# A graph network's first pass over the edges: a batch's sums are added in four quarters between VectorE's compares

## The chip, the cores and the metric

The kernel runs on one core of one Trainium2 chip. The metric is the device time of one execution in microseconds, the median of several runs. The core has TensorE (PE, with weight loads shown apart as PEld), VectorE (DVE), ScalarE (ACT), GpSimd (POOL) and SyncE (SP), which mostly issues DMAs.

## What is computed

Four layers of a graph network run one after the other over 6250 nodes with 64 features and 200000 edges, sorted by target node. The first one is the one that matters here:

```python
h = jnp.maximum(_layernorm(x, axis=-1), 0.0)
msg = jnp.concatenate([h[src], edge_features], axis=1)      # 200000 x 96
agg = jax.ops.segment_sum(msg, dst, num_segments=6250)
x = x + relu(jnp.concatenate([h, agg], axis=1) @ W.T + b)
```

The second and the fourth layer are attention layers over the same edges, the third one a weighted sum. The first layer's pass over the edges also builds two tables of one-hots (of a source node's low and high part) that the third layer reads later.

## The kernel before

The edges are cut into 392 batches of 512 (four tiles of 128). `sum_sweep` is the first layer's pass. Each engine runs its own list of stages through `pipeline(eng, stages, unroll)`: at step t it does, in the order of the list, each stage (lag, stage) for batch t - lag. Two times 16 steps are written out, the rest is a loop of 16 steps a turn, and the last steps are written out again. So the order of the list is the order of the engine's instructions, and a wait in a stage holds all that stands behind it.

In a step the engines do this:

- POOL (`gather_stage`, L780): four indirect DMAs fetch the rows of a batch's 512 source nodes into one of 8 buffers, once PE has summed the batch that used the buffer before. One batch in eight (`looked_up`, slot 3) needs none, since its rows come from the look-up below.
- ScalarE: `join` (L1055) puts the edge features beside the rows; `hots` (L1072, L1076) makes the node one-hots of 17 tiles of nodes.
- PE: `sums` (L1092) adds up the batch with four f32 matmuls, in one of four PSUM banks, then `lookups` (L1100): for every eighth batch the rows are found by one-hot matmuls instead of a gather, spread over eight batches. A batch has four look-ups with one-hots of VectorE and two of ScalarE (three in one slot), in this order: two of VectorE, one of ScalarE, two of VectorE, one of ScalarE. Each look-up is four matmuls.
- VectorE: `build` (L1131) compares the target nodes of batch t; `low` (L1152) and `high` (L1161) make batch t - 2's part of the tables for later; `add` (L1141) takes batch t - 6's sums from PSUM and adds them to 128 columns of `accT` in SBUF, at a window whose start is in a register; `hots` (L1176) makes four node one-hots for batch t - 6's look-ups; `fill` (L1190) reduces the two banks of a finished look-up, in one step of eight.
- SP: loads of edge features (L1005), of the source lines that `low` reads (L1014), of the indices (L791), of the look-up line (L1040), and the store of the tables (L1024). `line` and `keep` wait for `low` and `high`.

`add` and the four `hots` are of the same batch: PE's look-ups of batch b need hots(b), these stand behind add(b), and add(b) waits for PE's sums(b). The four hots have four buffers, and each waits until PE has used the one before it in its buffer.

VectorE's list before is

```python
pipeline(dve, [(0, build), (2, low), (2, high), (6, add), (6, hots), (7, fill)], unroll=GATHER_UNROLL)
```

Of the kernel before, what the change touches and what calls it, by code (L numbers as in the profile page):

```python
# [19 lines left out]


# [1 line left out]

# [1 line left out]

# [7 lines left out]
ALU = mybir.AluOpType  # L33
# [24 lines left out]
WINDOW, WINDOW_STEP = 128, 64  # L58
# [9 lines left out]
LOOK_EVERY, LOOK_AT = 8, 3  # L68
# [4 lines left out]
GATHER_UNROLL = 2 * IDX_GROUP  # L73
# [48 lines left out]
def done(eng, sem, b):  # L122

    eng.wait_ge(sem, b.v + 1)


def free(eng, sem, b, ring):

    if not b.early(ring):
        eng.wait_ge(sem, b.v + (1 - ring))  # L130
# [28 lines left out]
def pipeline(eng, stages, unroll=UNROLL):  # L159

    def step(i, t):
        for lag, stage in stages:
            b = t - lag
            if i is not None or 0 <= b < N_BATCHES:
                stage(Batch(i, b, unroll))
    last = (N_BATCHES - 1) // unroll
    for t in range(2 * unroll):
        step(None, t)
    with eng.bass.Fori(2, last, engines=(eng.engine,), head_slot={eng.engine: 0}) as i:
        for u in range(unroll):  # L170
            step(i, u)
    for t in range(last * unroll, N_BATCHES + max(lag for lag, _ in stages)):
        step(None, t)
# [63 lines left out]
def graph_layers(nc, a, out):  # L237
    ctx = contextlib.ExitStack()
    with ctx:
        def sb(name, shape, dt=F32):  # L240
# [44 lines left out]
        accT = wide_room[:, 0:N_PAD]  # L285
# [105 lines left out]
        dve_bases, dve_late_bases, pe_bases = (  # L391
            Bases(eng, name, base) for eng, name in ((nc.vector, "now"), (nc.vector, "late"),
                                                     (nc.tensor, "pe")))
# [521 lines left out]
        def sum_sweep(name):  # L915


            width = sum_width

            def sweep():  # L920
                with Phase(nc, name) as ph:
                    s_onehot, s_joined, s_sum, s_added, s_low, s_high = (
                        ph.sem(n) for n in ("onehot", "joined", "summed", "added", "low", "high"))
# [37 lines left out]
                    def onehots_of(b):  # L961
                        slot = b.slot(SUM_RING)
                        t = onehot if slot < RING else onehot_wide
                        return t[:, slot % RING, :, :]

                    def sum_bank(b):
                        return banks[b.slot(RING)][0:width, 0:P]
# [10 lines left out]
                    def hots_dve(b):  # L978
                        n = HOTS_DVE // LOOK_EVERY
                        return range(n * b.slot(LOOK_EVERY), n * (b.slot(LOOK_EVERY) + 1))  # L980
# [9 lines left out]
                    @block.gpsimd  # L990
                    def _(pool):
                        pipeline(pool, [(0, gather_stage(pool, node_rows, sum_rows[:, :, :, 0:D], s_rows, s_idx,
                                                         [s_sum], some_looked_up=True))],
                                 unroll=GATHER_UNROLL)
                        end_gathers(pool, some_looked_up=True)
# [130 lines left out]
                    @block.vector  # L1126
                    def _(dve):
                        def build(b):
                            free(dve, s_sum, b, SUM_RING)
                            wide = [P, TILES_PER_BATCH, P]  # L1130
                            dve.tensor_tensor(  # L1131
                                onehots_of(b), iota[:, :].unsqueeze(1).to_broadcast(wide),
                                tiles_of(dst_rel, b).unsqueeze(2).to_broadcast(wide),
                                ALU.is_equal).then_inc(s_onehot, 1)

                        def add(b):
                            at = accT[0:width, bass.ds(dve_bases.of(b), WINDOW)]
                            done(dve, s_sum, b)
                            if not b.early(1):
                                dve.wait_ge(s_added, b.v)  # L1140
                            dve.tensor_tensor(at, sum_bank(b), at, ALU.add).then_inc(s_added, 1)  # L1141

                        def hot_of(b):
                            return hot_out[:, b.of_group(EDGE_GROUP).slot(2), b.slot(EDGE_GROUP), :]

                        def low(b):
                            slot = b.of_group(EDGE_GROUP).slot(2)
                            landed(dve, s_line, b.of_group(EDGE_GROUP), 16)
                            if not b.early(2 * EDGE_GROUP):
                                dve.wait_ge(s_kept[slot], b.of_group(EDGE_GROUP).uses(2) * 16)  # L1150
                            wide = [P, BATCH // 2, 2]
                            dve.tensor_tensor(  # L1152
                                hot_of(b)[:, 0:BATCH].rearrange("p (e t) -> p e t", t=2),
                                low_line[:, slot, b.slot(EDGE_GROUP), :].rearrange(
                                    "p (e t) -> p e t", t=2),
                                lane_pair[:, :, :].to_broadcast(wide),
                                ALU.is_equal).then_inc(s_low, 1)

                        def high(b):
                            wide = [P, TILES_PER_BATCH, NODE_TILES]  # L1160
                            dve.tensor_tensor(  # L1161
                                hot_of(b)[:, BATCH:HOT].rearrange("p (g j) -> p g j", j=NODE_TILES),
                                iota_b[:, 0:NODE_TILES].unsqueeze(1).to_broadcast(wide),
                                tiles_of(src_high, b).unsqueeze(2).to_broadcast(wide),
                                ALU.is_equal).then_inc(s_high, 1)
                        def hots(b):
                            if not has_lookup(b):
                                return
                            if b.slot(LOOK_EVERY) == 0:
                                landed(dve, s_look, b.of_group(LOOK_EVERY), 16)  # L1170
                            before = block_of(b) * HOTS_DVE
                            for n in hots_dve(b):
                                if n >= 4 or not b.early(LOOK_EVERY):
                                    dve.wait_ge(s_used_dve, before + n - 3)
                                wide = [P, BATCH // 2, 2]
                                dve.tensor_tensor(  # L1176
                                    dve_hots[:, n % 4, :].rearrange("p (e t) -> p e t", t=2),
                                    look_in(b).rearrange("p (e t) -> p e t", t=2),
                                    node_pairs[:, n:n + 1, :].to_broadcast(wide),
                                    ALU.is_equal).then_inc(s_hot_dve, 1)  # L1180

                        def fill(b):
                            if b.slot(LOOK_EVERY) != LOOK_EVERY - 1 or not has_lookup(b):
                                return
                            to = b.later(LOOK_AT + 1)
                            dve.wait_ge(s_used_dve, (block_of(b) + 1) * HOTS_DVE)
                            dve.wait_ge(s_used_act, (block_of(b) + 1) * HOTS_ACT)
                            dve.wait_ge(s_sum, to.v + (1 - ROW_RING))
                            for h, bank in enumerate(look_banks(b)):
                                last = dve.reduce_sum(  # L1190
                                    sum_rows[:, LOOK_AT, 2 * h:2 * h + 2, 0:D],
                                    bank[:, 0:2 * PARTS * D].rearrange(
                                        "p (g n d) -> p g d n", n=PARTS, d=D), AX)
                            last.then_inc(s_filled, 1)
                        c = Chain(dve, s_parts)
                        for tiles in src_groups:
                            value = of_tiles(normed, tiles)
                            left = parts_left.rearrange("p (j d) -> p j d", d=D)[:, 0:len(tiles), :]
                            parts = [parts_of(tiles)[:, :, n, :] for n in range(PARTS)]
                            c.do(split(dve, c, value, left, parts))  # L1200
                        pipeline(dve, [(0, build), (2, low), (2, high), (6, add), (6, hots), (7, fill)],
                                 unroll=GATHER_UNROLL)
            windows_loop(name, sweep, [next_places])

        def kept_sum_sweep(name):
# [946 lines left out]
        low, high = slice(0, WINDOW_STEP), slice(WINDOW_STEP, P)  # L2152
# [172 lines left out]
```

## Time and profile before

| what | value |
|---|---|
| time, median of 3 runs | 7310.23 us (7301.25 to 7313.19) |
| span of the profiled execution | 8677.5 us |
| PE busy in the span | 4986.1 us, 57% |
| DVE busy | 4776.9 us, 55% |
| ACT busy | 4214.7 us, 49% |
| POOL busy | 5500.0 us, 63% |
| mean granted TensorE clock | 0.733 |

The profile is of one execution, whose span is 1367 us longer than the median of the timed runs. Busy time leaves out register, branch, semaphore and DMA-issuing instructions of all engines but POOL's indirect DMAs. In a timeline a row merges like instructions that follow one another; the bracket behind it is the engine's idle time before it and what ended it. "issue" is time in which the engine waited for nothing that the profile shows, "remote" a wait whose releaser it does not find.

### The profile page before, as it was taken

To read this page: it belongs to the slowest core of one execution; us is meant where nothing else is said; L and a number is where in the kernel's file an instruction comes from. 1 tells how busy PE (TensorE), PEld (TensorE's weight loads), DVE (VectorE), ACT (ScalarE), POOL (GpSimd) and SP (SyncE) were. 2 spreads that over 40 slices of the span, in tenths; PEclk is the share of its full clock that TensorE was granted. 3 is DMA by queue.
4 is the path that set the end of the run, shared out by engine and by line. 5 is a ranking of instruction groups with operands and counts; after the bars stand their busy time and mean duration, and the time that the engine had idled before them with its cause. 6 is when DMAs were issued, how large, how long until landed. Compare 5 with 4: busy or idle time off the path is not lost. (4 is left out here: it accounts for less than half of the span.)

```text
span 8677.5 us, 161248 instructions
## 1 busy us (share of the span) xinstructions
PE 4986.1 (57%) x37998; PEld 3663.8 (42%) x38194; DVE 4776.9 (55%) x21264; ACT 4214.7 (49%) x11640; POOL 5500.0 (63%) x5713
## 2 busy tenths in 40 slices
PE   4555555555564444444444447997566666666664
PEld 3455444554452222222222226885444444444443
DVE  5455444554444555555455558996555555555556
ACT  3455444554423433333333348994455554544544
POOL 6777777777745555555555556994555555555553
PEclk8788888888776666666666668998666666666666
DMA  3232322333224444444444446885222222222221
GB/s 113 79 85 84 85 78 84 85 84 85 78 77 128 128 127 125 126 124 128 124 125 128 126 130 195 268 268 211 57 60 62 62 62 61 60 61 61 62 61 43
DMA packets 672779, 908.53 MB, mean 105 GB/s; under 512 B 141174, under 2 KB 429928, under 8 KB 672441
## 3 DMA queue, kind: packets, MB, share of 16 engines
q1 hardware_dynamic: 502366, 605.50, 22.6%
q0 software_dynamic: 168944, 301.30, 14.2%
q8 instruction: 42, 0.69, 0.0%
q10 hardware_dynamic: 1357, 0.47, 0.0%
q14 instruction: 70, 0.57, 0.0%
HBM read 696.57 MB, written 210.28 MB: 105 GB/s over the span
## 5 line engine op out<-in xcount | busy, mean ns | idle before, releaser
L780 POOL DMA_INDIRECT rows<-src_rows,idx_slots x1563 | 1489.5, 953 | 1214.6 <-DVE pre L1487 667.1
L780 POOL DMA_INDIRECT rows<-node_rows,idx_slots x1371 | 1867.1, 1362 | 569.0 <-issue 363.9
L780 POOL DMA_INDIRECT rows<-rel_rows,idx_slots x1563 | 1482.7, 949 | 1093.8 <-remote 457.3
L1375 ACT ACTIVATE onehot<-ident,fresh_slots 128x128 f32<-128x128 f32 x3136 | 992.6, 387 | 969.1 <-remote 651.8
L1366 PE MATMUL bank<-onehot,ones 128*128 128x512 f32 x1568 | 1296.2, 922 | 114.5 <-ACT onehot L1375 52.6
L1100 PE MATMUL bank<-by_chunk,dst_pairs 128*128 128x192 bf16 x6144 | 714.8, 265 | 973.9 <-DVE dst_pairs L1176 716.1
L1463 PE MATMUL bank<-w_e,edge_in 128*128 128x256 f32 x784 | 442.0, 665 | 1403.0 <-DVE onehots L860 1070.7
L1072 ACT ACTIVATE dst_pairs<-pre,minus_node 128x512 bf16<-128x512 int16 x816 | 580.8, 720 | 1220.5 <-remote 660.3
L1100 PEld LDWEIGHTS bank<-by_chunk,dst_pairs 128*128 128x128 bf16 x6144 | 534.8, 105 | 1084.0 <-DVE dst_pairs L1176 783.6
L1463 PEld LDWEIGHTS bank<-w_e,edge_in 128*128 128x128 f32 x784 | 192.3, 299 | 1853.9 <-DVE onehots L860 887.1
L1141 DVE TENSOR_TENSOR wide_room<-bank,wide_room 96x128 f32 x392 | 112.6, 287 | 1258.5 <-remote 719.0
L1512 DVE TENSOR_TENSOR onehots<-bank,onehots 128x512 f32<-128x512 f32 x392 | 269.7, 688 | 936.6 <-remote 669.3
L1669 PE MATMUL bank<-rows,onehot 128*128 128x65 f32 x3136 | 599.2, 352 | 243.2 <-DVE wide_room L1762 205.6
L1609 ACT ACTIVATE shrink<-grown 128x1 f32<-128x1 f32 x392 | 79.5, 203 | 1215.0 <-DVE grown L1713 974.8
L1669 PEld LDWEIGHTS bank<-rows,onehot 128*128 128x128 f32 x3136 | 553.1, 265 | 259.9 <-issue 240.7
L1446 ACT ACTIVATE onehot<-onehots,exp_bias 128x512 bf16<-128x512 f32 x392 | 282.9, 722 | 677.7 <-DVE max_by_chunk L1544 286.4
L1176 DVE TENSOR_TENSOR dst_pairs<-pre,node_pairs 128x512 bf16<-128x512 int16 x1536 | 544.6, 414 | 0.0
L1076 ACT ACTIVATE dst_pairs<-dst_pairs,ones 128x512 bf16<-128x512 bf16 x816 | 540.7, 707 | 1.6
L1624 ACT ACTIVATE onehot<-onehots,edge_in 128x128 f32<-128x128 bf16 x1568 | 500.6, 389 | 20.0
L1294 ACT ACTIVATE onehot<-onehots,edge_scale 128x128 f32<-128x128 bf16 x1568 | 500.7, 390 | 12.6 <-DVE onehots L1349 12.5
L1100 PE MATMUL bank<-wide_room,dst_pairs 128*128 128x192 bf16 x3264 | 439.4, 261 | 35.0 <-ACT dst_pairs L1076 30.3
L1643 PEld LDWEIGHTS bank<-by_chunk,onehots 128*128 128x128 bf16 x3136 | 269.2, 125 | 417.4 <-issue 416.8
(304 smaller groups left out, 11860.9 us busy)
## 6 DMA issues: line engine op xcount, KB each, us to landing
edge_in<-dst_line SPq DMA_DIRECT2D x392, 256.0 KB
spill<-rows SPq DMA_DIRECT2D x392, 256.0 KB
rows<-spill SPq DMA_DIRECT2D x392, 256.0 KB, 3.2
hot_rows<-rows SPq DMA_DIRECT2D x98, 712.0 KB
onehots<-hot_rows SPq DMA_DIRECT2D x196, 356.0 KB, 3.5
onehots<-src_low SPq DMA_DIRECT2D x98, 512.0 KB
edge_in<-in_ea_l SPq DMA_DIRECT2D x98, 256.0 KB
edge_in<-in_eaT_l SPq DMA_DIRECT2D x392, 64.0 KB
```

The source lines that it names most:

```text
L780: pool.indirect_dma_start(out=to[:, b.slot(ROW_RING), g, :], out_offset=None, in_=table, in_offset=bass.IndirectOffsetOnAxis(ap=idx_slots[ ...
L1072: act.activation(act_hots[:, n % 2, :], look_in(b), ACT.Square, bias=minus_node[:, n:n + 1]).then_inc(s_square, 1)
L1076: act.activation(act_hots[:, n % 2, :], act_hots[:, n % 2, :], ACT.Relu, scale=-1.0, bias=ones[:, 0:1])\
L1100: last = pe.matmul(look_banks(b)[g // 2][:, at:at + PARTS * D], hot[:, g * P:(g + 1) * P], node_parts(j), start=(j == 0 and g % 2 == 0), s ...
L1176: dve.tensor_tensor(dve_hots[:, n % 4, :].rearrange("p (e t) -> p e t", t=2), look_in(b).rearrange("p (e t) -> p e t", t=2), node_pairs[:, ...
L1294: last = act.activation(onehot[:, b.slot(RING), g, :], plain_of(b)[:, g, :], ACT.Copy, scale=edge_scale[:, b.slot(RING), g:g + 1])
L1366: return pe.matmul(bank, ones[:, :], diag[:, b.slot(2), :, :].rearrange("p g e -> p (g e)"), start=start, stop=True)
L1375: last = act.activation(diag[:, b.slot(2), g, :], ident[:, :], ACT.Copy, scale=fresh_slots[:, b.slot(2 * RING), g:g + 1])
L1446: act.activation(exp_out, masked1[:, b.slot(2), :], ACT.Exp, bias=exp_bias[:, slot, :], accum_out=exp_sum[:, slot, :])
L1463: pe.matmul(to, edge_blocks[:, b.slot(RING), :], w1_e[:, :, :].rearrange("p g f -> p (g f)"), start=True, stop=False)
L1624: last = act.activation(weighted[:, b.slot(2), g, :], onehot_b[:, b.slot(ONEHOT_RING), g, :], ACT.Copy, scale=share[:, b.slot(RING), g:g + 1])
L1669: last = pe.matmul(summed, weighted[:, b.slot(2), g, :], rows[:, b.slot(ROW_RING), g, D:2 * D + 1], start=(g == 0), stop=(g == TILES_PER_B ...
```

## The change

`add` is cut into four instructions of 32 columns each, and `hots` into four stages of one compare each. The list of VectorE becomes: build(t), add0, hot0, add1, hot1 (all of t - 6), low(t - 2), add2, hot2, high(t - 2), add3, hot3, fill(t - 7). The wait for PE's sums stands at the first quarter, the semaphore `s_added` is raised by the last one. Nothing else is changed.

```diff
+                        added_at = [0]
+
+                        def add(b, quarter):
+                            n = WINDOW // 4
+                            if quarter == 0:
+                                added_at[0] = dve_bases.of(b)
+                                done(dve, s_sum, b)
+                                if not b.early(1):
+                                    dve.wait_ge(s_added, b.v)
+                            at = accT[0:width, bass.ds(added_at[0] + quarter * n, n)]
+                            last = dve.tensor_tensor(
+                                at, sum_bank(b)[:, quarter * n:(quarter + 1) * n], at, ALU.add)
+                            if quarter == 3:
+                                last.then_inc(s_added, 1)
...
-                            for n in hots_dve(b):
+                            for n in hots_dve(b)[which:which + 1]:
...
-                        pipeline(dve, [(0, build), (2, low), (2, high), (6, add), (6, hots), (7, fill)],
-                                 unroll=GATHER_UNROLL)
+                        pipeline(dve, [(0, build), (6, add0), (6, hot0), (6, add1), (6, hot1), (2, low),
+                                       (6, add2), (6, hot2), (2, high), (6, add3), (6, hot3),
+                                       (7, fill)], unroll=GATHER_UNROLL)
```

## Rows read from the trace of the kernel before

**Rows 1.** Windows: stretch, its length, each engine's busy time, PEclk, DMA share, GB/s

```profile
82.00:2481.00 2399.00, 1340.62 (x12536) 1205.50 (x12536) 1140.52 (x3184) 1158.03 (x2012) 1850.88 (x1354) 0.82 0.30 83
...
2626.00:5231.00 2605.00, 1222.29 (x6191) 640.30 (x6187) 1344.01 (x7394) 1034.75 (x3119) 1447.79 (x1519) 0.64 0.46 126
...
6101.00:8607.00 2506.00, 1558.34 (x10335) 1097.96 (x10529) 1359.83 (x8592) 1274.31 (x4300) 1452.46 (x1531) 0.68 0.23 61
```

**Rows 2.** The page's groups: busy, mean ns of one, idle before and releaser

```profile
L780 POOL DMA_INDIRECT rows<-src_rows,idx_slots x1563 | 1489.5, 953 | 1214.6 <-DVE pre L1487 667.1
```

**Rows 3.** Groups of instructions in 300 to 2300 us, inside the first layer's pass

```profile
L780 POOL DMA_INDIRECT rows<-node_rows,idx_slots x1144 | 1536.4, 1343 | 463.4 <-issue 300.2 <-PE bank L1092 83.1 <-remote 80.2
...
L1141 DVE TENSOR_TENSOR wide_room<-bank,wide_room 96x128 f32 x323 | 92.8, 287 | 1053.3 <-remote 655.4 <-PE bank L1092 329.3 <-issue 68.5
```

**Rows 4.** Timelines of DVE, PE and POOL, one quick turn: start, us, instruction, [idle before]

```profile
1223.70 0.29 DVE L1141 TENSOR_TENSOR wide_room<-bank,wide_room 96x128 f32 x1 [1.01 <-PE bank L1092]
1223.91 1.42 DVE L1176 TENSOR_TENSOR dst_pairs<-pre,node_pairs 128x512 bf16<-128x512 int16 x4
1225.25 0.68 DVE L1131 TENSOR_TENSOR onehots<-iota,dst_rel 128x512 f32<-128x512 f32 x1
1225.85 0.41 DVE L1152 TENSOR_TENSOR rows<-onehots,lane_pair 128x512 bf16<-128x512 bf16 x1
1226.19 0.36 DVE L1161 TENSOR_TENSOR rows<-iota_b,src_high 128x200 bf16<-128x200 bf16 x1
1227.55 0.29 DVE L1141 TENSOR_TENSOR wide_room<-bank,wide_room 96x128 f32 x1 [1.00 <-PE bank L1092]
...
1224.38 0.84 PE L1100 MATMUL bank<-by_chunk,dst_pairs 128*128 128x192 bf16 x8 [0.81 <-DVE dst_pairs L1176]
...
1226.38 1.04 PE L1092 MATMUL bank<-onehots,rows 128*96 128x128 f32 x8
...
1223.82 0.94 POOL L780 DMA_INDIRECT rows<-node_rows,idx_slots  x1 [0.30 <-PE bank L1092]
1225.07 2.29 POOL L780 DMA_INDIRECT rows<-node_rows,idx_slots  x1 [0.31 <-issue]
```

**Rows 5.** Timeline ahead of the loop, when PE waits for rows

```profile
163.69 0.29 DVE L1141 TENSOR_TENSOR wide_room<-bank,wide_room 96x128 f32 x1 [3.59 <-issue]
...
164.96 2.39 POOL L780 DMA_INDIRECT rows<-node_rows,idx_slots  x1 [0.30 <-issue]
...
166.18 0.36 DVE L1161 TENSOR_TENSOR rows<-iota_b,src_high 128x200 bf16<-128x200 bf16 x1
...
170.19 0.29 DVE L1141 TENSOR_TENSOR wide_room<-bank,wide_room 96x128 f32 x1 [3.65 <-issue]
```

**Rows 6.** Timeline at a standstill of the loop

```profile
1269.34 0.29 DVE L1141 TENSOR_TENSOR wide_room<-bank,wide_room 96x128 f32 x1 [2.60 <-PE bank L1092]
...
1272.03 1.04 PE L1092 MATMUL bank<-onehot,rows 128*96 128x128 f32 x8
...
1285.85 0.29 DVE L1141 TENSOR_TENSOR wide_room<-bank,wide_room 96x128 f32 x1 [12.72 <-remote]
```

**Rows 7.** Timeline of a step with reductions behind the hots, 16 batches earlier

```profile
1170.98 0.29 DVE L1141 TENSOR_TENSOR wide_room<-bank,wide_room 96x128 f32 x1 [2.61 <-PE bank L1092]
1171.19 1.43 DVE L1176 TENSOR_TENSOR dst_pairs<-pre,node_pairs 128x512 bf16<-128x512 int16 x4
...
1172.00 1.11 POOL L780 DMA_INDIRECT rows<-node_rows,idx_slots  x1 [0.30 <-issue]
```

**Rows 8.** VectorE's timeline in an attention pass: short additions

```profile
3805.05 0.15 DVE L1535 TENSOR_TENSOR grown<-max_by_chunk,run_max 128x1 f32<-128x1 f32 x1
3805.11 0.15 DVE L1537 TENSOR_TENSOR top<-run_max,a_b 128x1 f32<-128x1 f32 x1
3805.18 0.35 DVE L860 TENSOR_SCALAR onehots<-edge_in,window_lane 128x512 bf16<-128x512 int16 x1
```

**Rows 9.** Window of the stretch in which PE waits for rows

```profile
157.00:177.00 20.00, 11.47 (x98) 9.81 (x96) 8.83 (x26) 9.83 (x18) 16.34 (x13) 0.91 0.16 44
```

More of the change, by code:

```diff
@@ L22 @@
 import contextlib
+import functools
 import numpy as np
@@ L1134, in build @@
                                 ALU.is_equal).then_inc(s_onehot, 1)
[L1136 to L1141, printed above, removed]
+                        added_at = [0]
[11 more added lines that the diff above has]
+                                last.then_inc(s_added, 1)
                         def hot_of(b):
@@ L1165, in high, with hots @@
                                 ALU.is_equal).then_inc(s_high, 1)
-                        def hots(b):
+                        def hots(b, which):
                             if not has_lookup(b):
                                 return
-                            if b.slot(LOOK_EVERY) == 0:
+                            if b.slot(LOOK_EVERY) == 0 and which == 0:
                                 landed(dve, s_look, b.of_group(LOOK_EVERY), 16)
                             before = block_of(b) * HOTS_DVE
-                            for n in hots_dve(b):
+                            for n in hots_dve(b)[which:which + 1]:
                                 if n >= 4 or not b.early(LOOK_EVERY):
@@ L1200, in _ @@
                             c.do(split(dve, c, value, left, parts))
-                        pipeline(dve, [(0, build), (2, low), (2, high), (6, add), (6, hots), (7, fill)],
-                                 unroll=GATHER_UNROLL)
+                        add0, add1, add2, add3 = (functools.partial(add, quarter=n)
+                                                  for n in range(4))
+                        hot0, hot1, hot2, hot3 = (functools.partial(hots, which=n)
+                                                  for n in range(4))
+                        pipeline(dve, [(0, build), (6, add0), (6, hot0), (6, add1), (6, hot1), (2, low),
+                                       (6, add2), (6, hot2), (2, high), (6, add3), (6, hot3),
+                                       (7, fill)], unroll=GATHER_UNROLL)
             windows_loop(name, sweep, [next_places])
```

## The prediction, made before the result was known

> **What bounds the kernel now.** I read the windows by stage first [rows 1]. The first layer's pass is the stretch 82 to 2481 us: 2399 us for 392 batches, 6.12 us a batch, and no engine is full in it (POOL 77% busy, PE 56%, DVE 48%). The two attention passes follow and nothing of them is touched. Two limits lie in this pass, and a third thing that is neither: standstills.
>
> The first limit is a ring between TensorE and VectorE. In the timeline of an undisturbed batch [rows 4] the reader is to follow one turn: the add at 1223.70 waits for PE's sums; the four node compares (hots) start 0.21 later; PE's look-ups start at 1224.38, when the first compare is there; they and the next sums keep PE busy until 1226.38 + 1.04 = 1227.42; the next add starts at 1227.55. A turn is 3.85 us. VectorE idles 1.00 of it, PE 0.81.
>
> The second limit is POOL, which issues a batch's row gathers: four a batch, none for every eighth batch, so 56 for 16 batches. One that nothing holds takes 0.94 and 0.30 pass before the next: 1.25 us, or 3.5 x 1.25 = 4.38 us a batch. Yet of the gathers in [rows 4] one takes 0.94 and the next 2.29. The second starts at 1225.07 in the last hot and ends at 1227.36, which is 0.81 after the end of the compare "high" (1226.19 + 0.36 = 1226.55); the 2.39 one in [rows 5] ends at 167.35, again 0.81 after high's end (166.54). So a gather whose start meets VectorE's unbroken run of hots, build, low and high (2.64 us, 1223.91 to 1226.55) is held until that run is over. The mean gather of this pass is 1343 ns, not 944 [rows 3]. In the ordinary turn POOL gets two gathers through in 3.85 us, while 3.5 a turn are wanted: the eight buffers of rows run empty. Once they are empty the batch looks as in [rows 5]: add to add 6.50 us (163.69, 170.19), PE waiting for rows, three gathers at 1.25 and one at 2.69 (2.39 + 0.30), together 6.44. That is this pass when POOL bounds it: 14 batches of 16 have gathers, 14 x 6.50 / 16 = 5.69 us a batch.
>
> The third thing is a standstill. In [rows 6] PE's sums start at 1272.03 and the profile has them take 1.04, but the add that waits for them starts at 1285.85, with 12.72 of idle put down to "remote". Of 1053 us that VectorE idles ahead of the add in 2000 us, 655 are put down to "remote" [rows 3], in most turns of the loop two waits in each 16 batches, at the same place. Sixteen batches take 1269.34 - 1170.98 = 98.4 us (6.15 each): some fourteen quick turns and two of 16 to 22 us. In these POOL catches up, so in the profile it is not the bound that it would be without them.
>
> **Are the standstills in the timed runs?** The timed median is 7310, the profiled span 8677.5, 1367 longer; something of the profile is not in the runs. Take the attention passes at POOL's own pace, 392 x 4 gathers x 1.25 (mean 0.95 [rows 2] and 0.30 between [rows 4]) = 1960 us each instead of 2605 and 2506. The rest of the span outside the three passes is 8677 - 2399 - 2605 - 2506 = 1167. There is left for the first pass 7310 - 1167 - 3920 = 2223 us, 5.67 a batch. That is what [rows 5] gave for a pass bound by POOL with no standstill (5.69). It is one fit and no proof, but I take it: in the timed runs POOL bounds the first pass.
>
> **The change, part by part.** *The add in quarters.* One add of 128 columns takes 0.29 and lets the next instruction start after 0.21 [rows 4]. The nearest rows below are additions of one column, 0.15 long with the next starting 0.06 to 0.07 later [rows 8]. Between them a quarter of 32 columns occupies 0.07 + (32/128) x 0.14 = about 0.10; bounds 0.07 and 0.21. Four are 0.42 instead of 0.21 (0.28 to 0.84), while VectorE has 1.00 idle in the quick turn and more in the slow one: the extra 0.2 costs nothing by itself. The base of the window is read once a batch as before, and the semaphore is raised by the last quarter.
>
> *The order.* Before: add, four hots, build, low, high. After: add0, hot, add1, hot, low, add2, hot, high, add3, hot, then build. This is in PE's ring, since PE wants the hots one after the other. From the add's start as zero, with steps of 0.335 (hot, low), 0.29 (high), 0.10 (quarter), 0.41 for a hot's length and 0.06 until PE has it [rows 4]: hots reach PE at 0.57, 1.01, 1.78 and 2.50. A look-up lasts 0.33 (six of them lie between 1224.38 and the sums at 1226.38). PE does hot 1 until 0.90, waits 0.11, does hot 2 and ScalarE's first until 1.67, waits 0.11, does hot 3 until 2.11, waits 0.39, does hot 4 and ScalarE's second until 3.16, then the sums until 4.20, and 0.13 to the next add: 4.33 us instead of 3.85. So the ring itself gets 0.48 longer. With quarters at 0.07 it is 4.2, at 0.21 4.8.
>
> *What lies behind the moved wait.* add0 waits for PE and now has low and high queued behind it, which went ahead of it before. SP's loads and stores (L1005, L1014, L1024, L791) wait for them, so they go out up to 3 us later. The lines that low reads are fetched four batches ahead and the indices too, some 17 us: covered, and if not, POOL would wait for indices. build keeps its place at the head of a step, six batches before its reader.
>
> *POOL's holds.* The one run of 2.64 us falls into four: hot (0.34), hot and low (0.67), hot and high (0.62), hot and build (0.94). Whether a held gather gets in at such a break is seen in [rows 7], the batch in which two reductions of a PSUM bank follow the hots: the gather of 1172.00 takes 1.11 and ends at 1173.11; 0.81 back is 1172.30, the end of the third hot and before the fourth is over (1172.62). With an instruction in the queue that reads only one tensor of SBUF, POOL gets in soon. The add is of that kind: gathers that start beside it take 0.94 (1223.82 in [rows 4]). A gather that starts at a random point of a turn of about 4.9 waits on average (0.34² + 0.67² + 0.62² + 0.94²) / (2 x 4.9) = 0.18 us; 3.5 of them 0.63. POOL then needs 4.38 + 0.63 = 5.0 us a batch; bounds 4.4 (no wait) and 5.69 (as before).
>
> **Sum.** POOL 5.0 against the ring's 4.33: POOL still bounds, 5.69 - 5.0 = 0.69 us a batch saved, 392 x 0.69 = 270 us: 7310 - 270 = 7040. If POOL needed no wait the ring (4.33) and POOL (4.4) would give 1.3 x 392 = 510, so 6800; PE's clock speaks against that end. In [rows 9] PE is busy 11.47 of 20 us and the granted clock is 0.91 of the higher level (2.4 GHz), so with pauses it already drops at times to 1.2 GHz; after the change PE is busy 3.03 of 5.0, 61%, and some batches will still run at the lower level, where PE's 3.03 become about 6.
>
> **Rules of the Trainium skill.** The rows show holds over a whole run of instructions. "SBUF — State Buffer", who interferes with whom, says that a VectorE instruction with two SBUF inputs contends with a GpSimd instruction that reads SBUF, and one with a single SBUF input does not; it also says the loser blocks until the instruction ends. By the first the trace agrees, and the change helps. By the second, taken alone, a gather would get in after each compare already; [rows 4] differ from that (held over four instructions). The page adds that tensor_tensor was not seen to stall DMA issue; the 2.29 us gather here says otherwise.
>
> **Rivals.** *B, the standstills are in the timed runs.* For it: they sit at the same place in every turn of the loop, which looks like the program and not like the recording. Then they are POOL's time to catch up, POOL is not the bound, and the ring's 0.48 is lost in each batch: 392 x 0.48 = +188, 7310 + 188 = 7500; somewhat less, 7460, where a longer turn shortens them. It decides once the two standstills are longer than about 22 us together in 16 batches: (16 x 4.33 + 22) / 16 = 5.7, the batch of before. Against it: the fit above. The Trainium skill's page "Runtime: NRT & Kernel Launch", instruction fetch mechanics, says a taken branch to code outside the fetched window stalls the engine; by that rule they would be real. *C, POOL is not let in.* The breaks are only about 0.1 long, a compare is queued behind each, and the gather waits for the end of build. Then the blocked run grows from 2.64 to 0.32 + 0.335 x 5 + 0.29 + 0.60 = 2.9 and the held batch from 6.50 to 6.75: 0.25 x 14/16 x 392 = +85, 7395. Against it: [rows 7]. *D, standstills of middle length (12 to 22 us in 16 batches).* Gain and loss cancel: -100 to +40.
>
> **Chances.** Forecast (A) 0.55; B 0.25; C 0.10; D 0.10. Range: A reaches from 6900 (4.65 a batch) to 7170, B to 7480: 6900 to 7480. A alone: 6900 to 7170. A measurement of this kernel tells about 0.2% (15 us) from no change. Faster by more: 0.55 of A and half of D, 0.60. Within: 0.05. Slower: B, C and a part of D, 0.35.
>
> **What would show it.** In the profile after: gathers of L780 near 1.0 to 1.1 us in the mean instead of 1343 ns (step POOL; still 1.3 or more means C). Quick turns of 4.33 in place of 3.85, with PE idle put down to L1176 in three places (step order). L780 with short waits for PE's sums, because its eight buffers are full earlier. If the standstills are still in the profile and only there, its span gets longer (16 x 0.48 = 7.7 us in 98.4) though the timed runs get shorter; if both get longer, it is B. A quarter over 0.2 us apart or a clock that stays at the lower level would put the time above the forecast.

## The result, and the profile after

Before takes 7308.89 us (median of 20 runs, 7290.22 to 7330.5), the changed kernel 7321.65 us (20 runs, 7308.02 to 7328.81). The ratio is 1.0018, 95% interval [1.0011, 1.0025]: slower by 13 us, 0.18%. The forecast was 7040. The time lies outside the range of the forecast's own case (A, 6900 to 7170), and inside the whole range (6900 to 7480) only because that was stretched for rival B, which is not what happened.

First the windows of the profile after, the three passes (columns as in [rows 1]):

```profile
82.00:2397.00 2315.00, 1610.28 (x12495) 1301.65 (x12496) 1225.03 (x4332) 1161.99 (x2012) 1904.95 (x1346) 0.84 0.31 86
2535.00:4655.00 2120.00, 1360.56 (x7838) 718.57 (x7839) 1472.21 (x7707) 1152.46 (x3520) 1588.91 (x1780) 0.70 0.64 173
5340.00:7250.00 1910.00, 1390.05 (x10174) 982.59 (x10365) 1302.48 (x8443) 1253.61 (x4228) 1434.18 (x1517) 0.78 0.30 79
```

The span is 7322.3 us, 1355 less than that of before's first profile, and all three passes are shorter than in [rows 1]. (The second and third stretch do not fit the attention passes closely: these last from 2513 to 4464 and from 5305 to 7243 us.) That is no work of the change. A new profile of the kernel before (the first experiment) has a span of 7317.3 us. The standstills of [rows 6] were in that one execution and not in the timed runs beside it, and the two new profiles are what may be compared. Their groups in 300 to 2300 us (columns as in [rows 3]), first before, then after:

```profile
L780 POOL DMA_INDIRECT rows<-node_rows,idx_slots x1177 | 1643.9, 1397 | 358.8 <-issue 353.0 <-PE bank L1092 5.8
...
L1100 PE MATMUL bank<-by_chunk,dst_pairs 128*128 128x192 bf16 x5369 | 686.7, 282 | 274.7 <-DVE dst_pairs L1176 274.7
...
L1141 DVE TENSOR_TENSOR wide_room<-bank,wide_room 96x128 f32 x336 | 96.6, 287 | 1006.5 <-PE bank L1092 1006.5
```

```profile
L781 POOL DMA_INDIRECT rows<-node_rows,idx_slots x1165 | 1646.6, 1413 | 355.0 <-issue 352.3 <-PE bank L1093 2.7
L1101 PE MATMUL bank<-by_chunk,dst_pairs 128*128 128x192 bf16 x5308 | 740.0, 282 | 318.6 <-DVE dst_pairs L1185 317.3
...
L1147 DVE TENSOR_TENSOR wide_room<-bank,wide_room 96x32 f32 x1328 | 241.0, 181 | 895.5 <-PE bank L1093 894.1
```

In both POOL is never without work: its gathers are 0.30 us apart, and only 3 to 6 of 2000 us are waits for PE. It sets the pace with 3.5 x (1.40 + 0.30) = 5.95 us a batch before and 3.5 x (1.41 + 0.30) = 6.0 after. From build to build a batch takes 5.96 us before and 6.01 after (mean of batches 60 to 370). The change did not shorten the gathers. Its other half is there: PE waits 318.6 instead of 274.7 us for the hots.

### The profile page after: what moved, and what is told of

It is laid out like the page before. It is cut to its first block and busy times, and to the rows that moved or that the text cites. A ratio compares the mean times of both kernels' runs of the same rounds, so it can differ in the third digit from the quotient of the medians.

```text
span 7322.3 us, 163600 instructions
## 1 busy us (share of the span) xinstructions
PE 5119.7 (70%) x37998; PEld 3629.9 (50%) x38194; DVE 4811.0 (66%) x22440; ACT 4195.7 (57%) x11640; POOL 5568.7 (76%) x5713
## 5 line engine op out<-in xcount | busy, mean ns | idle before, releaser
L781 POOL DMA_INDIRECT rows<-node_rows,idx_slots x1371 | 1929.4, 1407 | 439.5 <-issue 413.5
L1380 PE MATMUL bank<-onehot,ones 128*128 128x512 f32 x1568 | 1251.2, 893 | 132.2 <-ACT onehot L1389 123.9
L1101 PE MATMUL bank<-by_chunk,dst_pairs 128*128 128x192 bf16 x6144 | 857.4, 282 | 369.9 <-DVE dst_pairs L1185 368.5
L1147 DVE TENSOR_TENSOR wide_room<-bank,wide_room 96x32 f32 x1568 | 283.7, 182 | 1052.9 <-PE bank L1093 1051.2
L1185 DVE TENSOR_TENSOR dst_pairs<-pre,node_pairs 128x512 bf16<-128x512 int16 x1536 | 636.5, 414 | 7.0 <-issue 6.3
L1683 PE MATMUL bank<-rows,onehot 128*128 128x65 f32 x3136 | 538.6, 327 | 48.5 <-DVE wide_room L1776 46.3
L1501 DVE TENSOR_TENSOR pre<-bank,rows 128x256 f32<-128x256 f32 x392 | 165.9, 423 | 573.1 <-DMA rows<-src_rows,idx_slots 569.6
L1683 PEld LDWEIGHTS bank<-rows,onehot 128*128 128x128 f32 x3136 | 495.2, 240 | 64.4 <-issue 54.3
L1101 PE MATMUL bank<-wide_room,dst_pairs 128*128 128x192 bf16 x3264 | 476.4, 279 | 1.8 <-ACT dst_pairs L1077 0.6
L1699 DVE CUSTOM_DVE_ANT_0 pre<-bank,rows 128x64 f32<-128x64 f32 x1568 | 259.9, 221 | 318.0 <-DMA rows<-rel_rows,idx_slots 313.4
```

What stands on the lines that cost most here:

```text
L781: pool.indirect_dma_start(out=to[:, b.slot(ROW_RING), g, :], out_offset=None, in_=table, in_offset=bass.IndirectOffsetOnAxis(ap=idx_slots[ ...
L1101: last = pe.matmul(look_banks(b)[g // 2][:, at:at + PARTS * D], hot[:, g * P:(g + 1) * P], node_parts(j), start=(j == 0 and g % 2 == 0), s ...
L1147: last = dve.tensor_tensor(at, sum_bank(b)[:, quarter * n:(quarter + 1) * n], at, ALU.add)
L1185: dve.tensor_tensor(dve_hots[:, n % 4, :].rearrange("p (e t) -> p e t", t=2), look_in(b).rearrange("p (e t) -> p e t", t=2), node_pairs[:, ...
L1380: return pe.matmul(bank, ones[:, :], diag[:, b.slot(2), :, :].rearrange("p g e -> p (g e)"), start=start, stop=True)
L1683: last = pe.matmul(summed, weighted[:, b.slot(2), g, :], rows[:, b.slot(ROW_RING), g, D:2 * D + 1], start=(g == 0), stop=(g == TILES_PER_B ...
```

## Where a gather gets in

DVE's and POOL's timelines of a quick turn in the profile after, to be held against [rows 4]:

```profile
1204.21 0.19 DVE L1147 TENSOR_TENSOR wide_room<-bank,wide_room 96x32 f32 x1 [1.30 <-PE bank L1093]
1204.32 0.42 DVE L1185 TENSOR_TENSOR dst_pairs<-pre,node_pairs 128x512 bf16<-128x512 int16 x1
1204.66 0.18 DVE L1147 TENSOR_TENSOR wide_room<-bank,wide_room 96x32 f32 x1
1204.77 0.41 DVE L1185 TENSOR_TENSOR dst_pairs<-pre,node_pairs 128x512 bf16<-128x512 int16 x1
1205.10 0.41 DVE L1161 TENSOR_TENSOR rows<-onehots,lane_pair 128x512 bf16<-128x512 bf16 x1
...
1206.58 0.68 DVE L1132 TENSOR_TENSOR onehot<-iota,dst_rel 128x512 f32<-128x512 f32 x1
1208.56 0.19 DVE L1147 TENSOR_TENSOR wide_room<-bank,wide_room 96x32 f32 x1 [1.31 <-PE bank L1093]
...
1205.28 2.79 POOL L781 DMA_INDIRECT rows<-node_rows,idx_slots  x1 [0.30 <-issue]
1208.38 0.94 POOL L781 DMA_INDIRECT rows<-node_rows,idx_slots  x1 [0.30 <-issue]
```

The turn is 4.35 us (1204.21 to 1208.56), predicted 4.33; a quarter and the compare behind it are 0.11 apart, predicted 0.10. But the gather of 1205.28 ends at 1208.07, and 0.81 back is 1207.26 = 1206.58 + 0.68, the end of build. It waited through the rest of low, two hots, high, two quarters and build. The reader can see why the quarter is no break: the first hot ends at 1204.32 + 0.42 = 1204.74, the quarter started at 1204.66, before that end, and the next hot starts at 1204.77. Between the two compares lie 0.03 us (0.02 in most places; without a quarter the next compare starts 0.08 before the end of the one ahead, [rows 4]). In 300 to 2300 us, 324 of before's 1176 gathers take 1.5 us or more (mean 2.56), and 318 of the 1165 after (mean 2.59). Between 1.0 and 1.5 us there are 31 before and 118 after: mostly gathers that started in the first hot and got in at its end, or in build, behind which VectorE is idle.

For the question at which boundary between two compares a waiting gather gets in, I took every gather of 1.03 us or more that starts in 300 to 1800 us and counted the ends of compares that it waited through and the one at which it got in (its own end less 0.81). Ends within 0.10 us of a gather's start are left out, and so is the end of a run, behind which VectorE is idle. Of the changed kernel and the four kernels made from it the table has only the boundaries with something between the compares; where two compares still overlap in them, 2 gathers got in and 434 ends were waited through (changed) and 15 and 675 (quarters alone). By the gap, from the end of one compare to the start of the next:

| kernel | gap and what is in it | got in | waited on |
|---|---|---|---|
| before, again | -0.08, nothing | 15 | 907 |
| changed | 0.02 to 0.03, a quarter | 36 | 376 |
| quarters alone | 0.02 to 0.03, a quarter | 84 | 152 |
| before, waits behind 6 compares | 0.03, VectorE waits | 146 | 0 |
| the same | 0.12 to 0.22, VectorE waits | 213 | 0 |
| before, waits behind the hots | 0.03 to 0.27, VectorE waits | 364 | 0 |
| the same | -0.08, nothing | 53 | 0 |
| before, waits behind build and low (a run with standstills, below) | 0.03 to 0.04, VectorE waits | 191 | 0 |
| the same | -0.08, nothing | 16 | 697 |
| changed, copy 96x32 | 0.12, quarter and copy | 257 | 2 |
| changed, copy 96x128 | 0.22, quarter and copy | 260 | 0 |
| changed, second add | 0.22, quarter and second add | 255 | 0 |

## Experiments

Where nothing else is said the result is unchanged by the edit. The mean gather and the us a batch (build to build, batches 60 to 370) are from each profile, gathers in 500 to 1500 us.

| kernel | us, before beside it | ratio, 95% interval | mean gather, ns | us a batch |
|---|---|---|---|---|
| before, again | 7319.13, 7301.57 | one run | 1394 | 5.96 |
| changed | 7321.65, 7308.89 | 1.0018 [1.0011, 1.0025] | 1413 | 6.01 |
| quarters alone | 7261.12, 7301.57 | 0.994 [0.9927, 0.9952] | 1389 | 5.91 |
| order alone | 7318.25, 7301.57 | 1.0021 [1.0012, 1.003] | 1419 | 6.03 |
| before, waits behind 6 compares | 6784.98, 7301.57 | 0.9288 [0.9274, 0.9301] | 1020 | 4.64 |
| before, waits behind the hots | 6783.37, 7315.99 | 0.9271 [0.9256, 0.9287] | 1006 | 4.60 |
| changed, copy 96x32 in 3 breaks | 7002.56, 7311.59 | 0.9574 [0.9558, 0.959] | 1179 | 5.17 |
| changed, copy 96x128 in 3 breaks | 7108.05, 7315.99 | 0.9715 [0.9698, 0.9731] | 1266 | 5.51 |
| changed, second add in 3 breaks | 7101.31, 7311.59 | 0.9712 [0.9696, 0.9728] | 1261 | 5.49 |
| changed, waits behind hots, low, high | 7170.59, 7311.59 | 0.9809 [0.9792, 0.9825] | 988 | 5.68 |

**The kernel before, once more**, to see whether the standstills belong to it.

> The kernel before once more, unchanged, for a profile. If the standstills of the first profile belonged to that execution alone, the span is about 7310 us, the first pass lasts about 2220 us, gathers of the pass take about 1.4 us in the mean and the steady batch is 6.5 us from add to add. If they belong to the program, two of 16 to 22 us stand in each 16 batches again.

Span 7317.3 us, no idle time put down to "remote" ahead of the add (the row above; it was 655.4 in [rows 3]), 5.96 us a batch. POOL bounds the first pass, as the forecast's fit had said; rival B, which needed the standstills in the timed runs, falls for these runs.

**The change's two parts, one at a time.** Quarters alone: the list is build, low, high, add0, hot0, add1, hot1, add2, hot2, add3, hot3. Order alone: add stays whole.

```diff
-  pipeline(dve, [(0, build), (2, low), (2, high), (6, add), (6, hots), (7, fill)],
+  pipeline(dve, [(0, build), (6, add), (6, hot0), (6, hot1), (2, low),
+                 (6, hot2), (2, high), (6, hot3), (7, fill)],
```

> Quarters alone: build, low and high keep their old place ahead of the add; the four quarters alternate with the four hots. Theory Q (a held gather waits for every compare that VectorE's queue already holds, and a quarter between them does not let it in): the run that holds a gather grows by three quarters of 0.10, the time stays or rises by up to 0.3 x 14/16 x 392 = 100 us. Theory G (the quarters let gathers in, the new order ate the gain): faster by 100 us or more, mean gather below 1.2 us.

> Order alone: the add stays whole, low and high go between the hots. Theory Q: the run that holds a gather keeps its 2.64 us, POOL still bounds, within 20 us of before. Theory G (order costs PE's ring 0.4 us a batch): slower by more than 60 us.

Quarters alone are 40 us faster, which neither of its theories had; order alone is 17 slower, as theory Q said; the sum would be -23 and both together are +13, so they are not additive. Neither moves the mean gather by more than 25 ns. With the quarters alone, 49 gathers of 500 to 1500 us, which started in the first hot, end 0.81 behind its end (mean 1.05 us), but of the 159 that started in a later hot 132 are held to the end of high (2.1 to 3.2 us) and 26 to the end of the last hot.

**VectorE waits for its own compare**, in the order of before, behind hots, build and low, then behind the hots only. The edit puts a real gap between two compares:

```diff
                                     ALU.is_equal).then_inc(s_hot_dve, 1)
+                                dve.wait_ge(s_hot_dve, before + n + 1)
...
                                 ALU.is_equal).then_inc(s_onehot, 1)
+                            done(dve, s_onehot, b)
...
+                            done(dve, s_low, b)
```

> The kernel before with a wait of VectorE for its own last compare behind every hot, build and low, so that the next compare is not in its queue while one runs. Theory Q: a gather gets in after one compare at most, mean gather about 1.1 us, the pass needs about 5.0 us a batch instead of 5.7, some 200 us faster, if VectorE's waits (some 0.1 each, 0.7 a batch) do not bound. Theory L (the port is held from the first to the last compare whatever is queued, or the gather waits for VectorE's idleness for another reason): gathers as before, time as before or up to 100 us slower.

> The kernel before with the waits behind the four hots only; build, low and high still follow one another unbroken (1.3 us). Theory Q: a gather that comes in the hots is let in after one, one that comes in the last compares waits for the end of high, up to 1.3: mean gather 1.1 to 1.2, time between drained (6785) and before (7302), near 6900.

Minus 7.1 and minus 7.3%, more than either expectation had. The shorter gathers account for it: 3.5 x (1.394 - 1.020) = 1.31 us a batch with six waits, against 5.96 - 4.64 = 1.32, so nothing is left for the clock to explain. Groups of the kernel with six waits, 500 to 1500 us, and its timeline:

```profile
L780 POOL DMA_INDIRECT rows<-node_rows,idx_slots x756 | 770.8, 1020 | 230.4 <-issue 226.7 <-PE bank L1092 3.7
...
L1142 DVE TENSOR_TENSOR wide_room<-bank,wide_room 96x128 f32 x216 | 61.9, 287 | 101.4 <-PE bank L1092 101.2
```

```profile
843.70 1.79 DVE L1178 TENSOR_TENSOR dst_pairs<-pre,node_pairs 128x512 bf16<-128x512 int16 x4
845.63 0.69 DVE L1131 TENSOR_TENSOR onehots<-iota,dst_rel 128x512 f32<-128x512 f32 x1
...
843.93 0.99 POOL L780 DMA_INDIRECT rows<-node_rows,idx_slots  x1 [0.30 <-issue]
845.23 1.07 POOL L780 DMA_INDIRECT rows<-node_rows,idx_slots  x1 [0.30 <-issue]
```

The hots end at 845.49 and build starts at 845.63, 0.14 later; between two hots the gap is 0.03, and four of them take 1.79 instead of the 1.42 of [rows 4], 0.12 more for each wait between them. No gather of the pass takes 1.5 us any more: the longest wait is for the end of the compare in progress. So the holds were what the forecast took them for, and worth more than it thought (517 and 533 us). What the change lacked was a gap that lets them in.

With the waits behind the hots only, build, low and high still overlap, and the expectation had gathers held there to the end of high. Yet of the gathers that started in build 53 got in at an overlapped end. So a gap behind the compare is not always needed.

Which gathers get in at a gap of 0.02 to 0.03 with a quarter in it can be told more closely. A gather that started in the first hot behind VectorE's idle time got in at its end each time (25 of 25 in the changed kernel, 79 of 79 with quarters alone). All others got in at such a gap 16 times and waited through it 528 times. In the kernel before, where the second hot overlaps the first, the gathers that started in the first compare behind idle time got in at its end in 4 of 50 cases. That is a pattern of these traces, not a cause shown.

**The ring by itself.** Before and the changed kernel, both with one gather a batch in the first pass instead of four; PE's sums then take the rows of the first tile for all four, so the first layer's sums are others.

```diff
-        return TILES_PER_BATCH
+        return GATHERED[0]     # 1 in sum_sweep("sum0")
...
-                                last = pe.matmul(sum_bank(b), sum_rows[:, b.slot(ROW_RING), g, :],
+                                last = pe.matmul(sum_bank(b), sum_rows[:, b.slot(ROW_RING), 0, :],
```

> The kernel before with one gather a batch in the first pass instead of four (all four sum matmuls read the first tile's rows, so the first layer's sums are of other rows). POOL then needs 1.25 to 2.7 us a batch and cannot bound. Step 'order' of the prediction: turns of 3.85 us from add to add.

> The changed kernel with one gather a batch, likewise. Step 'order': turns of 4.33 us, 0.48 longer than those of ring_before, with PE waiting for the hots in three places; the pass 392 x 0.48 = 190 us longer than that of ring_before. If the ring were not touched by the order, both passes are alike.

6548.62 and 6755.61 us, one run each: 207 us or 0.53 a batch for the change (predicted 0.48 and 188). Batches take 4.03 and 4.57 us, ordinary turns 3.85 and 4.35. The second kernel's timeline of PE has the waits where the prediction put them. Each row joins the matmuls of one look-up or two, so the waits show in the starts: the first two look-ups take 0.93 instead of the 0.84 of [rows 4], and those of the third and the fourth hot start 0.43 and 0.71 after the row ahead where 0.33 would do. That is 0.09, 0.10 and 0.38, predicted 0.11, 0.11 and 0.39:

```profile
1226.01 0.93 PE L1104 MATMUL bank<-by_chunk,dst_pairs 128*128 128x192 bf16 x8 [0.73 <-DVE dst_pairs L1188]
1226.78 0.49 PE L1104 MATMUL bank<-wide_room,dst_pairs 128*128 128x192 bf16 x4
1227.21 0.51 PE L1104 MATMUL bank<-by_chunk,dst_pairs 128*128 128x192 bf16 x4
1227.92 0.50 PE L1104 MATMUL bank<-by_chunk,dst_pairs 128*128 128x192 bf16 x4 [0.21 <-DVE dst_pairs L1188]
```

**How long must a break be, and of what kind?** The changed kernel with one more instruction behind quarters 2, 3 and 4, into unused SBUF: a copy of 96x32 from PSUM, a copy of 96x128, or a maximum of 96x128 that reads PSUM and SBUF.

```diff
+                            if quarter:
+                                last = dve.tensor_copy(
+                                    parts_left[0:width, quarter * P:(quarter + 1) * P], sum_bank(b))
```

> The changed kernel with a copy of the whole bank (96 x 128, PSUM to SBUF) behind the second, third and fourth quarter: breaks of 0.10 us become about 0.31. Theory Q (the compares already queued count): gathers are still held to the end of build; the run is 0.6 longer, so time rises by 0.6 x 14/16 x 392 = 200 us or up to it. Theory W (the break was only too short): mean gather falls from 1.41 to 1.15 or less and the time does not rise.

> The changed kernel with the copy of 96x32 behind three quarters, once more. Its gathers were 1198 ns in the mean, 1266 with the copy of 96x128. Without standstills it should then be the faster of the two: 0.955 to 0.97 against 0.9715 (6980 to 7090). If the length is what helps, it is above 0.975. With standstills 0.98 to 0.99 again.

> The changed kernel with a second 96x128 addition-like instruction (a maximum, PSUM and SBUF in) behind three quarters, once more. Its gathers were 1260 ns, as with the copy of the same size (1266), so without standstills the same ratio as there, 0.97 to 0.98 (7080 to 7150). If what reads SBUF holds POOL longer, 0.99 to 1.00. With standstills 0.985 to 0.995 again.

DVE and POOL of the kernel with the short copy:

```profile
1206.19 0.41 DVE L1164 TENSOR_TENSOR rows<-onehots,lane_pair 128x512 bf16<-128x512 bf16 x1
1206.53 0.18 DVE L1147 TENSOR_TENSOR wide_room<-bank,wide_room 96x32 f32 x1
1206.63 0.18 DVE L1150 COPY rel_biases<-bank 96x32 f32<-96x32 f32 x1
1206.73 0.41 DVE L1188 TENSOR_TENSOR dst_pairs<-pre,node_pairs 128x512 bf16<-128x512 int16 x1
...
1206.34 1.26 POOL L781 DMA_INDIRECT rows<-node_rows,idx_slots  x1 [0.30 <-issue]
```

low ends at 1206.60, the next hot starts at 1206.73: a gap of 0.13, and the gather gets in at the end of the copy (0.81 back from its end at 1207.60 is 1206.79; with the long copy and the maximum it is the end of the quarter, 0.09 behind the compare's). The same quarters with 0.02 to 0.03 between the compares let in few. So three instructions of 0.10 a batch turn 1.0018 into 0.957, without any wait. The long copy and the maximum, with gaps of 0.22, give the same time as each other (0.9715, 0.9712; gathers 1266 and 1261 ns): whether the filler reads one tensor of SBUF or none makes no difference. Longer than needed is worse, by some 100 us. One reason is in sight, though not tested alone: the fillers stand in the ring, and the phase of the requests shifts so that with the long copy 133 gathers in 500 to 1500 us start in the last hot and are held to the end of build (1.76 us each), which is the one place left without a gap.

**Both: the changed kernel with waits** behind each hot, low and high.

> The changed kernel with the waits behind hots, low and high, once more, for a comparison in which before takes near 7300. If the ring of the change bounds once the holds are gone: 4.7 to 5.2 us a batch, 6830 to 7000, ratio 0.935 to 0.96, against the 0.929 of the kernel before with waits. If POOL bounds both: 0.927 to 0.930. With standstills (before over 8500) 1.013 to 1.016 again.

```profile
L781 POOL DMA_INDIRECT rows<-node_rows,idx_slots x616 | 608.7, 988 | 389.6 <-PE bank L1093 208.8 <-issue 180.8
...
L1101 PE MATMUL bank<-by_chunk,dst_pairs 128*128 128x192 bf16 x2828 | 366.6, 254 | 346.4 <-DVE dst_pairs L1187 345.8 <-issue 0.7
```

The gathers are nearly as short as unheld ones (988 ns), yet the kernel is 386 us slower than the kernel before with its waits (0.9809 against 0.9288 of before), and slower than expected. POOL now waits 208.8 us in 1000 for PE, and PE 345.8 for the hots: the ring bounds, with ordinary turns of 5.39 us. Its timeline shows a quarter and a hot every 0.67 us, which were 0.44 apart without the waits, because a quarter can no longer start ahead of the end of the compare before it. The change's longer ring is a second loss, which POOL's holds cover in the changed kernel. By itself it is the 207 us of the ring test; the rest of the 386 comes with the waits, which lengthen this ring more than that of before.

**Comparisons in which the standstills are there.** In two of the comparisons the kernel before itself took 8558.82 us (14 runs, 8526.14 to 8586.11) and 8655.81 us (7 runs, 8642.54 to 8670.59), near the span of the first profile. It is not a matter of the chip alone: one and the same chip gave 7301.57 in one comparison and 8655.81 in another. In these runs:

| kernel | us | ratio, 95% interval | before |
|---|---|---|---|
| changed | 8709.35 | 1.0056 [1.0037, 1.0075] | 8655.81 |
| before, waits behind 6 compares | 8716.37 | 1.0061 [1.0038, 1.0084] | 8655.81 |
| before, waits behind build and low | 8504.45 | 0.9941 [0.9927, 0.9955] | 8558.82 |
| changed with waits | 8683.81 | 1.0155 [1.0116, 1.0195] | 8558.82 |
| changed with waits | 8782.59 | 1.0136 [1.0111, 1.0162] | 8655.81 |
| changed, copy 96x32 | 8422.82 | 0.9843 [0.9804, 0.9882] | 8558.82 |
| changed, second add | 8468.74 | 0.9901 [0.9865, 0.9937] | 8558.82 |

> The kernel before with VectorE's wait for its own compare behind build and low only, none behind the four hots (waits behind the four hots alone gave 6783, behind all six 6785). Theory R (the held time is that of the unbroken run that the gather meets: now hots and build together, 1.95 us instead of 2.64, then low and high alone): one held gather a batch ends about 0.65 sooner, 5.3 us a batch instead of 5.95, 7050 (7000 to 7120). Theory N (any wait in the turn is enough, since it lets POOL's queue catch up): 6780 to 6800.

> The changed kernel again, beside the two below on one chip. On a chip without standstills (before 7290 to 7330): 7310 to 7335, ratio 1.001 to 1.003. On one with standstills (before near 8560, as in the last four comparisons and as the span of the first profile): here rival B of the prediction holds in part. Theory: the holds cost less there, since POOL catches up in the standstills, and the ring's longer turn (4.36 against 3.85) shows in the quick turns, 1.00 to 1.02. Rival: POOL bounds there as well and the ratio is the same 1.002.

> The kernel before with the waits behind hots, build and low again. Without standstills 6780 to 6790, ratio 0.928. With standstills: the two waits of the loop stay, the gain is smaller, 0.93 to 0.96.

The same waits that give 7.1% give nothing here. Groups of the kernel before with waits, in this condition, 500 to 1500 us:

```profile
L780 POOL DMA_INDIRECT rows<-node_rows,idx_slots x549 | 531.7, 968 | 467.9 <-PE bank L1092 217.0 <-issue 135.0 <-remote 115.9
...
L1142 DVE TENSOR_TENSOR wide_room<-bank,wide_room 96x128 f32 x157 | 45.1, 287 | 339.7 <-remote 178.1 <-PE bank L1092 160.2 <-issue 1.4
```

The holds are gone (968 ns), POOL waits, and two turns in three are 6.5 us. VectorE's adds start on average 1.6 us after the recorded end of the sums that they wait for; without standstills it is 0.14 in before. VectorE gets PE's results later than PE's records would have it, and neither edit touches that. What it is, and why one comparison has it and another not, the traces don't show; it stays open. This is the condition that rival B spoke of. The changed kernel is 54 us slower there, not 188; its gathers are held as before (1420 ns) and POOL waits for PE 51 us of 1000 at most, so POOL still sets most of the pace. That the 54 us are the ring's is likely and not shown. The wait behind build and low alone was run only here, so its expectation without standstills (7050) has no answer. Its held gathers (141 in 500 to 1500 us that started in the hots) end 0.81 behind the end of build, 2.35 us, instead of behind high: with VectorE's waits the hold lasts until the first of them, wherever that is (191 got in there, none waited through).

## Why the prediction missed

**POOL bounds the first pass; the standstills are not in the timed runs.** Right for the runs that count, with the fit [rows 2, 5] as the only evidence. The batch was 5.96, not 5.69: the mean gather was 1397 ns, and the 1343 of [rows 3] came from a pass in which POOL had caught up at times. The fit's first pass of 2223 us was 2320 (82 to 2402 us of the new profile of before), while the attention passes took 3890 together (2501 to 4453 and 5298 to 7237 us) for 3920, and the rest 1106 for 1167. The conclusion held, but that 5.67 and 5.69 agreed so closely was luck: the pass took 5.92 us a batch, and 5.96 in its steady part.

**The quarters' cost, the ring.** Right: 0.10 to 0.11 a quarter, a turn of 4.35 for 4.33, three waits of PE in their places, +207 us for +188 where the ring bounds.

**POOL's holds: this step failed.** It said that the run of 2.64 falls into four and that a held gather gets in at each break, 3.5 gathers at 0.18, and so 5.0 us a batch for POOL. The runs show 6.01: gathers are held to the end of build (318 of 1165, 2.59 us in the mean), and the mean gather is 1413 ns where 1.0 to 1.1 us was forecast. The evidence was one gather, that of [rows 7], which got in at the end of the third hot, with the fourth 0.08 into it. Counted over 300 to 1800 us of the same trace, such a gather is an exception: held gathers got in at an overlapped end 16 times and waited through 783. Fifteen of the sixteen are about 98 us apart, one in every 16 batches, in the very step of [rows 7]; the step was looked at because it was special, and taken for the rule. The reductions behind the hots can't be what let it in, since the fourth hot came first; what did, no trace shows. The second half of the argument, that an instruction with one tensor of SBUF lets POOL in, was taken from gathers that start beside an add (0.94), where VectorE had idled before. And the gap that a quarter would leave could be had from [rows 4]: compares start 0.335 apart and last 0.41, so they overlap by 0.08, and a quarter of 0.10 leaves 0.02. That sum was made for the ring and not for the gap.

**Rival C was the mechanism, with a smaller price.** The gather waits for the end of build (2.79 us), as C said. It was priced at +85 us and came to +13. It took one held gather for each batch that has gathers, and that is about right: 318 in 2000 us, in which some 333 batches run and seven in eight of them gather. But it had that gather get 0.25 longer, and the held ones went from 2.56 to 2.59 in the mean. It also left out that gathers which start in the first hot get in at its end (with quarters alone the kernel is 40 us faster). It had a chance of 0.10; the count of the exceptions would have made it the likeliest.

**The rule behind the kind of break.** The prediction set the rule of the Trainium skill's page "SBUF — State Buffer", who interferes with whom (two SBUF inputs contend), beside the trace and let it decide the kind of break. The runs agree that the compares hold POOL. The same page says that the loser blocks until the instruction ends; the trace differs for compares that overlap or have only a quarter between them (the gather of 2.79 us waits through four ends of compares) and agrees where VectorE waits between them (0 of 359 waited on).

## What to carry to other kernels

Before counting on a break in an engine's run, work out the gap it leaves: the next start less the end of the instruction ahead. Here a break that only just outlasted the overlap of two queued instructions helped little. And count a pattern over the whole trace before a sum rests on it. Here the cheapest remedy was not to move work but to let VectorE wait for its own compare (four waits, -7.3%, 6783.37 us; six waits give the same). And ask of each reordering what it costs once its cover is gone: the ring's +0.5 us a batch was hidden by the very stall that the change was meant to remove. It is 207 us where POOL has little to do, and with the waits, which lengthen this ring further, the kernel stands 386 us behind the one with the old order.

## What was not expected

- VectorE's own wait lets a held gather in at a gap of 0.03 us, each time; a quarter with 0.02 to 0.03 around it does so in 120 of 648 cases, 104 of them at the first hot's end. Whether the hundredth of a microsecond or the quarter in flight makes the difference was not separated.
- A wait of VectorE for its own last compare costs 0.12 us between hots; a quarter and a hot behind such a wait take 0.67 instead of 0.44.
- With the holds gone the granted clock of TensorE (share of 2.4 GHz) rose: 0.83 in 500 to 1500 us before, 0.95 with the waits, where PE is busy 739.5 instead of 673.0 us of the 1000, and 1.00 with one gather a batch (774.9 us busy). A matmul of the look-ups fell from 284 to 256 ns.
- The same kernel takes 7300 or 8600 us, and an edit that gives 7% in one condition gives none in the other. A profile whose span lies 1367 us above the timed median says so at once, and its waits should be re-taken before they are read.
